# Attention and a mixture of experts on one core: rows loaded two experts ahead, a lead of seven tiles, and four smaller edits

## The reference

```python
xn = _layernorm(x, axis=-1)
q, k, v = ((xn @ w.T + b).reshape(B, T, H, Dh) for w, b in ((wq_w, wq_b), (wk_w, wk_b), (wv_w, wv_b)))
scores = jnp.einsum('bthd,bshd->bhts', q, k) * Dh ** (-0.5)
scores = jnp.where((xn[:, :, 0] != 0)[:, None, None, :], scores, -jnp.inf)
attn = jnp.einsum('bhts,bshd->bthd', softmax(scores), v).reshape(B, T, C) @ wo_w.T + wo_b
# experts: the two best of 8 logits, at most cap = 1280 tokens each
logits = xn @ gate_w                       # masked to the two best, softmax -> router_probs
exp_batches = einsum('nec,nd->ecd', sec_mask, xn)
h = gelu_exact(einsum('ecd,edh->ech', exp_batches, c_fc) + fc_bias)
exp_out = einsum('ech,ehd->ecd', h, c_proj) + proj_bias
out = x + attn + einsum('nec,ecd->nd', cb_weight, exp_out)
```

## Time and profile before

| | us |
|---|---|
| median of the 3 runs shown | 716.48 |
| the 3 runs | 718.2, 716.48, 712.72 |
| the profiled execution | 716.14 |
| its span | 714.3 |
| PE busy | 618.3 (87%) |
| DVE busy | 406.7 (57%) |
| ACT busy | 394.9 (55%) |
| POOL busy | 229.0 (32%) |

### The profile page before, as it was taken

One profiled execution on the slowest core, in us unless ns is written; L12 is line 12 of the kernel. 1 busy time (PEld: TensorE's weight loads), 2 busy tenths in 40 slices (PEclk: granted clock), 3 DMA queues, 4 the chain that ended last, 5 costly groups with the idle time before them and its releaser, 6 DMA issues.

```text
span 714.3 us, 9757 instructions
## 1 busy us (share of the span) xinstructions
PE 618.3 (87%) x3526; PEld 322.6 (45%) x3526; DVE 406.7 (57%) x601; ACT 394.9 (55%) x775; POOL 229.0 (32%) x230
## 2 busy tenths in 40 slices
PE   4767999599999999989778867969999999899884
PEld 2433443223333343358767766869334333224312
DVE  5758598458888979831111110111798988857602
ACT  3442067357778877883144134323877787655751
POOL 3856911623343431200110011010255566322310
PEclk9989599759999999999789989889999999756955
DMA  6887044211212121422133033211312122111120
GB/s 191 248 277 233 21 180 155 72 38 51 73 54 74 59 68 39 119 67 74 34 107 104 27 84 108 64 45 38 102 47 76 48 73 80 58 43 27 47 66 15
DMA packets 57999, 60.44 MB, mean 85 GB/s; under 512 B 8032, under 2 KB 42848, under 8 KB 57952
## 3 DMA queue, kind: packets, MB, share of 16 engines
q1 hardware_dynamic: 52160, 45.92, 21.3%
q0 software_dynamic: 5792, 13.90, 6.3%
HBM read 29.65 MB, written 29.62 MB: 83 GB/s over the span
## 4 chain that ended last, share of the span: by engine, by line
PE 52%; DVE 21%; DMA 8%; ACT 6%; SPq 5%; issue 4%; POOL 1%; another core or an unknown queue 1%; DVEq 0%; POOLq 0%; ACTq 0%
DVE nmax L765 14%; PE bPV L983 14%; PE bX L967 12%; PE bD L1074 12%; DMA xe<-slot_x 5%; PE bD L948 5%; ACT probs L621 4%; PE bPV L1109 2%; PE bX L957 2%; DMA k_rows<-hid 2%; PE bD L991 1%; PE bD L1002 1%; DVE ye L808 1%; SPq L368 1%; DVE attn L783 1%
## 5 line engine op out<-in xcount | busy, mean ns | idle before, releaser
L765 DVE TENSOR_REDUCE nmax<-bD 128x2 f32<-128x1024 f32 x256 | 300.5, 1218 | 76.5 <-PE bD L948 58.7
L621 ACT ACTIVATE probs<-bX 128x512 f32<-128x512 f32 x512 | 268.2, 597 | 114.7 <-PE bX L967 102.6
L967 PE MATMUL bX<-Q,K 27*128 27x512 f32 x512 | 186.4, 503 | 19.0 <-ACT probs L621 12.6
L983 PE MATMUL bPV<-probs,v_aug 128*32 128x512 f32 x1024 | 152.0, 668 | 1.6 <-ACT probs L621 0.7
L967 PEld LDWEIGHTS bX<-Q,K 27*128 27x128 f32 x512 | 76.0, 196 | 163.5 <-ACT probs L621 111.3
L948 PE MATMUL bD<-K,Q 25*128 25x512 f32 x512 | 137.2, 508 | 10.7 <-DVE nmax L765 7.4
L1074 PE MATMUL bD<-wpj,hid 128*128 128x128 f32 x640 | 88.2, 306 | 11.4 <-DVE xeT_lo L798 6.3
L1074 PEld LDWEIGHTS bD<-wpj,hid 128*128 128x128 f32 x640 | 85.8, 220 | 14.8 <-issue 14.8
L512 POOL DMA_INDIRECT slot_x<-xn_all,put_i x64 | 62.4, 975 | 90.3 <-PE bPV L983 76.4
L649 ACT ACTIVATE hid<-bX,fcb 128x512 f32<-128x512 f32 (+1 forms) x96 | 55.5, 615 | 47.1 <-PE bX L1063 46.5
L948 PEld LDWEIGHTS bD<-K,Q 25*128 25x128 f32 x512 | 58.6, 197 | 47.1 <-DVE nmax L765 29.8
(11 more groups left out here) (104 smaller groups left out, 488.3 us busy)
## 6 DMA issues: line engine op xcount, KB each, us to landing
K<-k_rows SPq DMA_DIRECT2D x128, 50.0 KB
Q<-q_rows SPq DMA_DIRECT2D x128, 48.0 KB
slot_x<-hid POOLq DMA_DIRECT2D x10, 512.0 KB, 3.0
xe<-slot_x SPq DMA_DIRECT2D x8, 640.0 KB, 6.3
slot_y<-ye SPq DMA_DIRECT2D x8, 640.0 KB, 4.3
q_rows<-hid SPq DMA_DIRECT2D x8, 512.0 KB, 3.7
k_rows<-hid SPq DMA_DIRECT2D x8, 512.0 KB, 5.4
acc<-in_x SPq DMA_DIRECT2D x8, 256.0 KB, 4.9
```

The lines of the kernel that those rows point to most:

```text
L621: taken(nc.scalar.activation(probs[:, (g % 2) * 4 + i, :], next_x()[:], ACT.Exp, scale=SCALE))
L765: nc.vector.tensor_reduce(nmax[q][:, k, 2 * pair:2 * pair + 2], bank()[:], AX.X, ALU.max, negate=True).then_inc(s_dd, 1)
L967: filled(nc.tensor.matmul(next_x()[:], K[u][rows_used, q, j * P:(j + 1) * P], Q[u][rows_used, q, :], start=True, stop=True))
L983: last = nc.tensor.matmul(bPV[32 * h:32 * h + 32, :], v_aug[b % 2][:, j, u * UH + QUAD * q + h, :], probs[:, (g % 2) * 4 + h, :], start=(g ...
```

## The change

- **Expert rows.** SP asks for the rows of expert e + 2 as soon as those of e + 1 are out of xe, ahead of the store of the results of e and of the weights of e + 2. The rows of expert 1 are asked for before the loop.
- **Zero fill.** The ten DMAs alternate between two semaphores, and POOL waits for the one before the last, so two are in flight. The add of bo is made in eight parts, one for each batch, after puts 1, 3, 5 and so on to 15, and `take_out(b)` waits for its part. `put_after` goes from group 1 to 56 in place of 4 to 55.
- **Combinations.** Those of batches 4, 5 and 6 on DVE move from groups 105, 112 and 119 to 109, 116 and 123.
- **Full products.** In the groups of the last batch that have no tile ahead, PE issues two products of ones_r and hot into the second half of the free bank of bD.
- **Maxima.** LEAD is 7: one tile less in the lead-in, and each tile is issued one group later.
- **Lead-in.** Eight products in place of three ahead of the first pair of tile 2.

```diff
--- before.py
+++ after.py
@@ -46,7 +46,7 @@
 UNITS = H // UH
 GROUPS = 2 * TT
 GB = UNITS * GROUPS
-LEAD = 8
+LEAD = 7
 HALVES = 2 * UNITS
 QUAD = 4
 STRIP = P // QUAD
@@ -74,7 +74,7 @@
 
 def put_after(i):
 
-    return 4 + i * (GROUPS_BEFORE - 16) // KN
+    return 1 + i * (GROUPS_BEFORE - 12) // KN
 
 
 def got_after(i):
@@ -82,7 +82,7 @@
     return GROUPS_BEFORE + 1 + i * (B * GB - GROUPS_BEFORE - 4) // KN
 
 
-COMBINED_AT = {GROUPS_BEFORE + 9 + 7 * b: b for b in range(COMBINED_BY_POOL, B - 1)}
+COMBINED_AT = {GROUPS_BEFORE + 13 + 7 * b: b for b in range(COMBINED_BY_POOL, B - 1)}
 
 
 class Count:
@@ -261,7 +261,7 @@
         s_xe = sem("s_xe")
         s_xhi = sem("s_xhi")
         s_split = sem("s_split")
-        s_zero = sem("s_zero")
+        s_zero = [sem("s_zero0"), sem("s_zero1")]
         s_slot = sem("s_slot")
         s_get = [sem(f"s_get{b}") for b in range(B)]
         s_comb_p = sem("s_comb_p")
@@ -372,10 +372,12 @@
             def experts():
                 sp.wait_ge(s_put, KN * 16)
                 load_rows(0)
+                sp.wait_ge(s_dd, rows_item(0, NCH - 1) + 1)
+                load_rows(1)
                 for e in range(E):
-                    if e < E - 1:
-                        sp.wait_ge(s_dd, rows_item(e, NCH - 1) + 1)
-                        load_rows(e + 1)
+                    if e + 2 < E:
+                        sp.wait_ge(s_dd, rows_item(e + 1, NCH - 1) + 1)
+                        load_rows(e + 2)
                     sp.wait_ge(s_dd, results_end(e))
                     sp.dma_start(slot_y_v[e], ye[:]).then_inc(s_slot, 16)
                     if e + 2 < E:
@@ -498,13 +500,13 @@
                 pool.wait_ge(s_wr[b], WR_DMAS * 16)
             per = SLOTS * C // P // ZERO_DMAS
             nc.gpsimd.memset(hid_f[:, 0:per], 0.0).then_inc(s_fill, 1)
-            pool.wait_ge(s_xn, B)
-            nc.gpsimd.tensor_tensor(acc[:], acc[:], bo_s[:, None, :].to_broadcast([P, NT, C]), ALU.add).then_inc(s_bo, 1)
             pool.wait_ge(s_fill, 7)
             for h in range(ZERO_DMAS):
                 pool.dma_start(slot_x.rearrange("(p h r) c -> h p (r c)", p=P, h=ZERO_DMAS)[h], hid_f[:, 0:per]
-                               ).then_inc(s_zero, 16)
-                pool.wait_ge(s_zero, h * 16 + 16)
+                               ).then_inc(s_zero[h % 2], 16)
+                wait(pool, s_zero[1 - h % 2], (h + 1) // 2 * 16)
+            pool.wait_ge(s_xn, B)
+            pool.wait_ge(s_zero[(ZERO_DMAS - 1) % 2], ZERO_DMAS // 2 * 16)
             for k in range(TOPK):
                 for n in range(NT):
                     col = k * NT + n
@@ -512,6 +514,10 @@
                     pool.indirect_dma_start(slot_x, bass.IndirectOffsetOnAxis(ap=put_i[:, col:col + 1], axis=0),
                                             xn_all[:, n, :], None, bounds_check=SLOTS - 1, oob_is_err=False
                                             ).then_inc(s_put, 16)
+                    if col < 2 * B and col % 2 == 1:
+                        b = col // 2
+                        nc.gpsimd.tensor_tensor(rows(acc, b), rows(acc, b), bo_s[:, None, :].to_broadcast([P, TT, C]),
+                                                ALU.add).then_inc(s_bo, 1)
             for e in range(E):
                 q = e % 2
                 pool.wait_ge(s_w[q], e // 2 * 64 + 64)
@@ -785,7 +791,7 @@
                 d.step()
 
             def take_out(b):
-                dve.wait_ge(s_bo, 1)
+                dve.wait_ge(s_bo, b + 1)
                 take()
                 nc.vector.tensor_tensor(rows(acc, b), bank()[:, 0, :].rearrange("p (k c) -> p k c", c=C), rows(acc, b), ALU.add
                                         ).then_inc(s_dd, 1)
@@ -911,6 +917,7 @@
             products(B - 1, 1)
 
             d = Count()
+            hot_f = hot[:].rearrange("p n e -> p (n e)")
 
             def free():
 
@@ -1016,6 +1023,8 @@
                         scores_for_max(b, head // UH, head % UH, pair)
                     elif not last:
                         scores_for_max(b + 1, 0, head - GB, pair)
+                    else:
+                        nc.tensor.matmul(free()[:, 1, :], ones_r[:], hot_f, start=True, stop=True)
 
                 if g % 4 == 1 and not (last and g // 4 == 3):
                     maxima(b * HALVES + g // 4 + 1, (g // 4 + 1) % 2)
@@ -1099,7 +1108,6 @@
             pe.wait_ge(s_prefix, 1)
             pe.wait_ge(s_xT, B)
             pe.wait_ge(s_hot, 1)
-            hot_f = hot[:].rearrange("p n e -> p (n e)")
             nc.tensor.matmul(bX[1][:], prefix_r[:], hot_f, start=True, stop=True)
             nc.tensor.matmul(bPV[:], ones_r[:], hot_f, start=True, stop=True).then_inc(s_rank, 1)
 
@@ -1113,7 +1121,7 @@
                     pe.wait_ge(s_ranks, 1)
                 for pair in range(2):
                     if s >= 2:
-                        keep_clock(3)
+                        keep_clock(8 if (s, pair) == (2, 0) else 3)
                     scores_for_max(0, 0, s, pair)
                 if s == 5:
                     maxima(0, 0)
```

## The result

| | before | after |
|---|---|---|
| median, us | 717.34 (712.72 to 748.0, 4 runs) | 748.20 (746.44 to 762.62, 4 runs) |
| ratio | | 1.044, 95% 1.037 to 1.052 |
| a second time | 718.82 (712.35 to 750.62) | 749.63 (726.62 to 772.58); 1.047, 95% 1.031 to 1.062 |
| the profiled execution | 716.14 | 762.62 |
| its span, mean clock | 714.3, 0.88 | 760.8, 0.78 |

The change makes the kernel slower, by 31 us, where 58 us less was forecast. The profiled execution is the longest of its four; the second measurement's profile (726.62 us, clock 0.85) is the shortest of its four and shows falls at the same kind of place, but less time at half clock. Three points of the order of time part the span: the first group, up(0) and up(7).

The account below looks back on a forecast made before the run. PE, DVE and ACT waiting for each other in every group, and the clock falls that follow, were taken to bound the kernel. 716.1 - 35 - 10.5 - 13 + 12.4 - 3 - 9 = 658.0 us, range 638 to 686.

Parts of the forecast that it names:

- LEAD 7: Attention's maxima steps: PE comes too early and waits for DVE, 0.4 x 31 steps = +12.4 us, bounds 0 and 17.
- waits at the maxima steps take the clock down: Rival, attention: waits at L957 in each turn halve the clock, about 1.5 us a group, up to 836 us; chance 0.04.
- Expert rows: Eight experts: rows asked for earlier, six periods of 19.7 instead of 25.5 us; -35 us, bounds 22 and 36.
- Lead-in: Before the first group: one tile less, clock held by five more products, wait of 0.8; -10.5 us, bounds -1 and -11.3.
- Zero fill and puts: Early attention: fills two at a time, puts from near 97 us, shorter burst, clock kept; -13 us, bounds 0 and 17.
- the stand: Early attention: PE, DVE and ACT stopped during back-to-back puts, ACT for 6.45 us; tied to the burst by coinciding ends.
- Combinations: Moved to groups 109, 116, 123: PE waits near 1.0 us; gain 11 if the clock holds, 0 if not; -3 taken.
- Full products: Last groups: two products fill PE's 0.69 us idle and hold the clock, groups 2.60 us apart; -9 us, bounds 0 and 9.2.

Follow-up runs that it names:

- e1: The changed kernel with LEAD back at 8 instead of 7, all other edits kept; 657.06 us.
- e12: The changed kernel (LEAD 7) with two unused products ahead of each maxima step and 16 instead of 4 ahead of the first group; 698.79 us.
- e5: The changed kernel (LEAD 7) with two full products, their result unused, ahead of each maxima step in the groups; 703.32 us.
- e6: The changed kernel (LEAD 7) with 16 instead of 4 products ahead of the first group; 745.21 us.
- e8: The changed kernel with LEAD 8 and the combinations back in groups 105, 112 and 119; 661.5 us.
- e10: The changed kernel with LEAD 8, each DVE combination in two halves two groups apart, and four products in group 0; 649.41 us.
- e3: The kernel before with only the expert rows loaded two ahead; 677.27 us.
- e7: The changed kernel with LEAD 8 and without the two products in the last groups; 666.96 us.
- e2: The kernel before with LEAD 7 alone; 780.55 us.
- e11: The kernel before with only the expert rows two ahead and the products in the last groups; 673.75 us.
- e9: The changed kernel with LEAD 8 and the zero fill, add and pace of the puts of before; 681.37 us.
- e13: The changed kernel with LEAD 8, the eight adds ahead of the puts and no put before group 14; 677.06 us.
- e1_again: The changed kernel with LEAD 8 measured a second time, no further edit; 659.21 us.

## Why the prediction was wrong, point by point

**LEAD 7: the step that failed.** It stood in the sum as +12.4 us, "0.4 x 31 maxima steps", delay alone, and what the wait does to the clock stood in the sum at nothing. Measured, it is some 90 us in the change (748.20 to 657.06) and 69.5 us alone. The mechanism of the wait was right: PE comes 0.5 us too early at L964 at every step where the clock is full, 18 of the 31, and its matmuls waited 12.3 us for DVE in all. The price was wrong twice. As delay a step costs more than 0.4 us: over a whole turn at full clock the groups of after lie 3.12 us apart against 2.96 of before and e1, which is 0.65 a step, or 20 us over 31, above the bound of 17. With the idle filled it is the same (e12, 3.12).

The larger part is the clock: 45 more groups at half clock than before, at about 1.5 us each, are 68 us. Profile against profile the account nearly closes. The two stretches of attention had mean clocks of 0.76 and 0.66 in after and 0.91 and 0.94 in e1, which is some 250 us more at half clock; as 55 groups at 1.6 us more each (4.56 against 2.96) these are 88 us. The delay at the 18 steps with full clock is 12. Of the 102.7 us between the two profiles that is 100. That e5 gave back 46 us by products which do nothing shows the clock's part by experiment. The rest, about 45 us over e1, divides in the same way: clocks of 0.90 and 0.83 are some 66 us more at half clock than in e1, 23 us, and the delay is some 17. These divisions are estimates from single profiles.

The rival "waits at the maxima steps take the clock down" is what happened, at the place and nearly by the price it named (4.56 us a group at half clock, 4.57 forecast). It had so little chance because "with them the clock stood at 1.00 for 50 groups", which was no evidence: in those 50 groups L957 had never waited for DVE. The evidence to go by was in the same trace, and the forecast named it: 0.69 us of idle a group took the clock down.

**Expert rows: right.** -35 forecast; -33.8 alone, and -36.6 between up(0) and up(7). What PE waits for in these periods now is DVE's low part of the rows, 7.2 us in six of them against 5.1 before, as the forecast said.

**Lead-in: right in itself, worth nothing in the end.** Forecast -10.5, measured -8.0 at the first group; the wait there was 1.80 us, within the bounds of 0 to 2, where 0.8 was taken. But whether the clock held is not the edit's alone. Of the 13 profiles of kernels with eight products it held in 9 (but for 4 us at most) and stayed at half in 4 (e6, e8, e10, e12); of the four without, it held in one (e3). And behind a held lead-in the clock fell in the first groups in all but one (e7), at LEAD 8 too, for which e1 and e8 stand, the same code up to there:

```profile
86.14 0.50 PE L974 MATMUL bX<-Q,K 27*128 27x512 f32 x1
...
90.04 1.93 PE L990 MATMUL bPV<-probs,v_aug 128*32 128x512 f32 x8
```

```profile
93.74 0.50 PE L974 MATMUL bX<-Q,K 27*128 27x512 f32 x1
...
97.59 1.07 PE L990 MATMUL bPV<-probs,v_aug 128*32 128x512 f32 x8
```

The first is e1 (lead-in held, groups at half clock from 90 us to 128), the second e8 (lead-in at half, groups at full clock). From the first group to up(0) e1 takes 215.7 us and e8 202.3, so that e8, 7.6 us later at the first group, is 5.9 earlier at up(0). The forecast had no such fall, and this is the second error, some 10 us: without LEAD's 12.4, and with the one lead tile that LEAD 8 keeps (2.6), its sum is 648 us, and e1 measured 657 and 659. PE's idle isn't what these first groups of e1 show ahead of the fall: from 78 us to 90 it had none over 0.2 us. Nor is a lead-in at half clock a guard: of the seven, those of e2 and e6 (LEAD 7) and e11 (LEAD 8) had the fall in the first groups, the four others not. Why it comes behind nine of the ten held ones stays open.

**Zero fill and puts: right, undersized.** -13 forecast with 17 as the bound; e9 and e13 say 18 to 24. The ten fills took 18.5 us (80.82 to 99.36) in place of 36.6, about the half that was taken. That the burst of puts brings the stand was only inferred from one coincidence; e13 made the burst anew without the old fill and the stand came with it. It isn't certain in each execution: of the six profiles with such a burst, three had a stand (before, e9, e13) and three had none (e2 and e11 with 7 puts in a row, e3 with 19 from 125.31 us). Of the eleven without a burst none had one.

**Combinations: right in size by the medians.** -3 forecast, 2 to 4 measured, within the spread; the profiles' 8 to 11 us from up(7) to the end (e8) leave room for more. The fall at the moved combination (1.40 us of idle in e1, not the 1.0 expected) came as the forecast feared.

**Full products: right under its condition.** -9 forecast, 8 to 10 by the medians at full clock. With the clock down already they add 1.4 us a group (5.48 against 4.06, as the value matmuls of 684.21 and 688.27 lie apart in the trace of before), which the forecast's bound of 0 had left out. At full clock these groups lie 3.12 us apart in e1 (630.57 and 633.69), not the 2.60 that the forecast wanted to see, against 4.06 without the products; so the order of time accounts for some 6 us and the halved projection, and the medians, taken beside different kernels before, for the rest.

## What to carry to other kernels

Where one engine is meant to run at full clock through hundreds of short groups, slack ahead of each recurring wait is worth more than its own length: here a slack of 2.07 us at the maxima step turned into a wait of 0.5, and cost some 90 us, not 12. Price a new recurring idle twice, as delay and as groups at half clock, and look in the trace for the shortest idle that took the clock down, not for a long stretch in which nothing waited. Products that do nothing help only where they stand ahead of the fall; behind it each takes 0.8 us of PE. And one profile doesn't settle a question of the clock: the same code had its falls in different places.

## What the runs showed of the hardware that was not expected

- Idle times of 0.52 and 0.53 us on PE, with dense work around them, were followed at once by half clock (508.29 and 150.06), and the same idle of 0.51 at 239.08 was not: 4 of 16 such waits in the trace of after.
- The clock also fell with no such idle: in e1 at 90 us and in e11 at 96, where PE's longest idle in the ten us ahead was 0.2.
- A fall isn't healed by work alone: in after the clock stayed at half for 17 to 67 us at a time in the attention with PE busy in nine tenths of it and more (170.3 to 228 us: 55.6 of 57.7), but for one fall of 3.4 us. In e1 and e1_again, one code, the fall behind the combination lasted 17 and 7 us.
- Single runs of one kernel lie 9 to 46 us apart, and the longer ones have the lower mean clock (e10: 639.89 us at 0.975, 681.8 at 0.905).
- Indirect DMAs issued by POOL every 1.27 us, 8 to 20 in a row, were followed in three profiles by a stand without a releaser on the core: of POOL, ACT and DVE for 2.4 to 2.9 us in e9, of ACT and DVE for 6.5 and 5.9 us in before, of ACT and DVE for 13.5 and 12.1 us in e13. In three others (7, 7 and 19 in a row) there was none. What in the chip is short then, no run shows.
- DVE's cast of 128x16 took 0.80 us beside a tensor operation of POOL, and 0.17 without.
